# One border between two parts of a mixture-of-experts layer moved from row tile 36 to 40, scatters allowed between two gathers of a batch, and a wait rule of the planner changed

## The chip, the cores and the metric

The kernel runs on one core of one Trainium2 chip. The metric is the device time of one execution in microseconds, measured as the median of several runs. Beside it the profiler records one execution, whose rows are quoted below.

## The reference, cut to what matters

6250 nodes with 256 features go through one layer. `xn` is the layer norm of `x`. To `x` are added a graph term (for each of 106250 edges, sorted by destination, the row `xn[src]` times the edge's weight, summed by destination, times a 256x256 matrix) and a linear-attention term over all rows. The result goes through a second layer norm, a gate that picks 2 of 16 experts for each row, and the two chosen feed-forward experts (256 to 512, relu, 512 to 256):

```
agg = segment_sum(xn[src] * edge_weight[:, None], dst)
x   = x + agg @ weight + mix(xn)
y   = layernorm(x)
topk_vals, topk_idx = top_k(y @ gate_w + gate_b, 2)
h   = relu(y @ w1[e] + b1[e]);  expert_out = h @ w2[e] + b2[e]
out = x + layernorm(y + sum over the two chosen e of w * expert_out) * gamma + beta
```

## The kernel before, in words

The rows are cut into 49 row tiles of 128. The edges are cut into 831 tiles of 128 edges, and 12 of these make a batch; there are 70 batches (numbered 0 to 69, the last one with only 3 tiles). For each tile of edges GpSimd (POOL) issues one indirect DMA at L861 that gathers 128 rows of the normed table into `ring`. `ring` holds two batches, so the gathers of batch b wait at L859 for the products of batch b-2. TensorE forms the sums of a batch (`edges`, L1518), ScalarE copies them, TensorE puts them in place (`place`, L1527), and VectorE adds them into `aggT`. Since the edges are sorted by destination, row tile q is complete after batch `complete(q)` (35: batch 52, 39: batch 58, 47: batch 69, 48: batch 70, that is after the last one).

As row tiles become complete, groups of two of them go through `mix` (both added terms), `gate` (second norm and choice of experts) and, once for each sub-part of row tiles (`SUB`), through `rank`, `slots`, `line` and `list`. These count on VectorE, with small products on TensorE, which slot each row gets in a buffer that is sorted by expert. `slots` of a sub-part ends with `slots_done` (L1343, just after the copy at L1340). POOL then scatters the sub-part's rows into the slots, two indirect DMAs for each row tile (`scatter`, L839). `list` writes which expert and which tile of 128 slots each visit has. A visit (`moe`) is one tile of 128 slots through its expert: SP loads the expert's two weight blocks (514 KB at L738 and 640 KB at L740, only where the expert is new in its buffer of three) and the tile's rows (L727), TensorE transposes (L1642) and multiplies (`layer1` L1654 with 16 products, `layer2` L1667 with 8), VectorE adds the bias (L1451) and ScalarE's queue stores the result. After the last sub-part of a part (`PT`) everything that is still unvisited in that part is visited; before that only tiles that are full. Since the number of tiles is known only at run time, the last visits of a part's list are guarded: the list has a first run and a second, short run (`leave`) that is skipped as a whole when its first entry is empty. All engines go through `left_out` then.

When all visits of a part have stored their results, POOL picks them up row tile by row tile (`pick`, L852, two indirect DMAs for each row tile), and VectorE finishes the rows (`fin1`, `fin2`, L1469 to L1499) in groups of two row tiles. SP stores them (L770). In the kernel before no pick stands ahead of the end of the gathers.

The order of all this work is fixed when the program is written, by `plan()`. It walks through the batches with fixed costs (a gather 1.254, a visit 3.9, a scatter DMA 1.28, and so on) and fills, for each batch, the list `SLOTS[b]` of work that the engines do after the edges of batch b, and the list `POOL_AFTER[b]` of scatters and picks that POOL issues after the gathers of batch b. `SLOTS[70]` is the tail. Work of a batch may run over the planned landing of the next one by `LAG` = 6.0, except in the last three batches, where a visit is placed only if it ends before the landing. Within the tail no visit is placed ahead of the last sub-part's slots. `send(s, b, done)` places the scatter of sub-part s after the first batch whose planned landing is at least `SPARE` = 4.0 past the planned end of `slots`. `runs()` works out how many visits each sub-part lists.

With `SUB = (0, 8, 16, 24, 30, 36, 42, 49)` and `PT = (0, 36, 49)` the sub-parts list 8, 16, 16, 12, 32+3, 4 and 33+4 visits (a second number is the guarded `leave` run). Row tiles 0 to 35 are part 0, row tiles 36 to 48 are part 1.

Of the kernel before, what the change touches and what calls it, by code (L numbers as in the profile page):

```python
# [18 lines left out]
NT = NC * CH  # L19
# [13 lines left out]
BT = GT * WIN  # L33
TILES = -(-EDGES // P)
NB = -(-TILES // BT)
# [14 lines left out]

PT = (0, 36, NT)
SUB = (0, 8, 16, 24, 30, 36, 42, NT)
NPART, NSUB = len(PT) - 1, len(SUB) - 1
MOST = max(b - a for a, b in zip(SUB, SUB[1:]))
SUB_PART = [max(p for p in range(NPART) if PT[p] <= a) for a in SUB[:-1]]
PART = [max(p for p in range(NPART) if PT[p] <= q) for q in range(NT)]
ROWS_OF = [min(N, PT[p + 1] * P) - PT[p] * P for p in range(NPART)]

# [9 lines left out]
def ends_part(s):  # L70
    return SUB[s + 1] in PT


def runs():

    out, at = [], 0
    for p in range(NPART):
        seen, floors = 0, []
        for s in range(NSUB):
            if SUB_PART[s] != p:  # L80
                continue
            rows = min(N, SUB[s + 1] * P) - PT[p] * P
            mostly = max(0, 2 * rows // TS - MOSTLY)
# [29 lines left out]
MG = 2  # L113
GROUPS = [(a + i, min(a + i + MG, b)) for a, b in zip(SUB, SUB[1:]) for i in range(0, b - a, MG)]
FG = 2
# [19 lines left out]
GATHER, SCATTER = 1.254, 1.28  # L135
EDGES_PE, KV_PE, MID_PE, MIX_PE, GATE_PE, TAKEN_PE, LEFT_PE = 2.4, 5.0, 18.0, 2.3, 0.01, 3.9, 0.5
RANK_PE, LAG, SPARE, LANDS = 0.7, 6.0, 4.0, 4.0

BEHIND, TOP_DVE, SLOTS_DVE, LINE_DVE = (6.0, 5.0), (7.0, 4.0), (11.0, 8.5), (7.0, 4.5)
EDGE_SPARE = 5.0  # L140
# [6 lines left out]
def plan():  # L147
# [3 lines left out]
    pool = [[] for _ in range(NB + 1)]  # L151
    kvs, mixes, gates, routes = list(range(NT)), list(range(len(GROUPS))), [], []
    tiles, not_before, sent, over = [], {}, {}, {}
# [3 lines left out]
    def transfers(w):  # L157
        a, b = (SUB[w[1]], SUB[w[1] + 1]) if w[0] == "scatter" else FIN[w[1]]
        return 2 * (b - a) * SCATTER

    def landing(b, k):

        return landed + sum(GATHER * BT + sum(transfers(w) for w in pool[i]) for i in range(b, k))

    def send(s, b, done):

        k = b + 1
        while k < NB and landing(b, k) < done + SPARE:
            k += 1
        sent[s] = min(k, NB)  # L170
        at = max(done, landing(b, k) if k < NB else 0.0)
        pool[sent[s]].append(("scatter", s))
        not_before[s] = at + sum(transfers(w) for w in pool[sent[s]]) + LANDS

    def chain(work, b):
# [57 lines left out]
    for b in range(NB):  # L233
        landed = max(landed, edges_at[b]) + GATHER * BT
        now = max(now, landed) + EDGES_PE
        edges_at.append(now)
        work = slots[b]
        for f, at in opened:
            if at == b:
                work.append(("fin1", f))  # L240
        if fins and PART[FIN[fins[0]][0]] in over and over[PART[FIN[fins[0]][0]]] < b and b + 5 < NB:
            buffer = len(opened) % EB
            if free_from[buffer] <= b + 1:
                f = fins.pop(0)
                pool[b + 1].append(("pick", f))
                opened.append((f, b + 3))
                free_from[buffer] = b + 5
        while now < landing(b, b + 1) + (LAG if b < NB - ON_TIME else 0.0):
            before = now
            if kvs:  # L250
                work.append(("kv", kvs.pop(0)))
                now += KV_PE
                if not kvs:
                    slots[b + 1].append(("mid", 0))
                continue
            if ("mid", 0) in slots[b + 1]:
                break
            if work == [("mid", 0)]:
                now += MID_PE
            now += chain(work, b)  # L260
            if b < NB - ON_TIME or now + TAKEN_PE + AHEAD < landing(b, b + 1):
                now += expert(work, b)
            if now == before:
                then = next_time()
                if then is None or then > landing(b, b + 1) - EDGE_SPARE:
                    break
                now = then
        work += [("fin2", f) for f, at in opened if at == b]
        landed += sum(transfers(w) for w in pool[b])
    tail, end = slots[NB], pool[NB]  # L270
    waiting, closing, dve = [], [], 0.0
    while mixes or gates or routes or tiles or fins or waiting or closing:
        before = now
        if routes and routes[0][0] == "slots" and now >= routes[0][2]:
            s = routes[0][1]
            end.append(("scatter", s))
            sent[s] = NB
            landed = max(landed, now + SLOTS_DVE[1]) + transfers(end[-1])
            not_before[s] = landed + LANDS
        now += chain(tail, NB)  # L280
        if last in sent:
            before_tile = now
            now += expert(tail, NB)
            dve = max(dve, before_tile) + (RESULT_DVE if now > before_tile else 0.0)
            if closing and dve < now + CLOSE_DVE:
                tail.append(("fin2", closing.pop()))
                dve += CLOSE_DVE
            if not closing and waiting and waiting[0][1] <= now and dve < now + CLOSE_DVE:
                closing.append(waiting[0][0])
                tail.append(("fin1", waiting.pop(0)[0]))  # L290
                dve += CLOSE_DVE
        while fins and len(waiting) + len(closing) < TB - 1 and PART[FIN[fins[0]][0]] in over:
            f = fins.pop(0)
            end.append(("pick", f))
            landed = max(landed, now + (4.0 if PART[FIN[f][0]] == NPART - 1 else 0.0)) + transfers(end[-1])
            waiting.append((f, landed + 3.0))
        if now == before:
            now += 0.5
        assert now < 5000.0
    return slots, pool  # L300


SLOTS, POOL_AFTER = plan()
ORDER = [w for s in SLOTS for w in s]
MIXES = [w[1] for w in ORDER if w[0] == "mix"]
# [48 lines left out]
def gps_layer(nc, x, src, dst, first_dst, edge_w, gnn_w, wkv, wq, wout, bout, gate_w, gate_b,  # L354
# [5 lines left out]
    with ExitStack() as ctx:  # L360
# [250 lines left out]
        def after(eng, s, n):  # L611

            if n > 0:
                eng.wait_ge(s, n)  # L614
# [176 lines left out]
        def _(pool):  # L791
# [18 lines left out]
            for s, t in dealt.items():  # L810
                m = DEALT[s]
# [31 lines left out]
            def pick(f):  # L843
# [6 lines left out]
                for n, q in enumerate(range(*FIN[f])):  # L850
                    for k in range(2):
# [2 lines left out]
                            in_offset=bass.IndirectOffsetOnAxis(ap=slot_i[:, k, q:q + 1], axis=0),  # L854
                        ).then_inc(picked[i], 16)

            pool.wait_ge(consts_in, 16 * len(CONSTS))
            for b in range(NB):
                after(pool, batch_done, b - 1)  # L859
                for m in range(min(BT, TILES - b * BT)):  # L860
                    pool.indirect_dma_start(  # L861
                        out=ring[:, b % 2 * BT + m, :], out_offset=None, in_=table,
                        in_offset=bass.IndirectOffsetOnAxis(ap=src_sb[:, b * BT + m:b * BT + m + 1], axis=0),
                    ).then_inc(gathered[b % 2], 16)
                for stage in POOL_AFTER[b]:
                    {"scatter": scatter, "pick": pick}[stage[0]](stage[1])
            for stage in POOL_AFTER[NB]:
                {"scatter": scatter, "pick": pick}[stage[0]](stage[1])

        @block.scalar  # L870
        def _(act):
# [897 lines left out]
```

## Time and profile before

| what | value |
|---|---|
| time of the kernel, median of 3 runs | 1505.05 us (1502.7 to 1506.33) |
| time of the profiled execution | 1499.34 us |
| its span, first to last instruction | 1497.4 us |
| mean granted TensorE clock | 0.868 |
| PE busy / POOL busy | 1019.7 us / 1005.2 us |
| gathers, first start to last end | 53.2 to 1245.4 us |
| first scatter of the last sub-part | 1280.5 us |

The profiler's busy time is a share of the whole span, which has three stages here: a first one of norms (to 53 us), the gathers (to 1245 us), and the tail. An engine's share says little; what each stage waits for is read from the waits and from the timeline. In rows of the timeline the first number is the start and the second the duration in us, and the bracket at the end gives how long the engine was idle before the instruction and what released it.

### The profile page before, as it was taken

To read this page: it belongs to the slowest core of one execution; us is meant where nothing else is said; L and a number is where in the kernel's file an instruction comes from. 1 tells how busy PE (TensorE), PEld (TensorE's weight loads), DVE (VectorE), ACT (ScalarE), POOL (GpSimd) and SP (SyncE) were. 2 spreads that over 40 slices of the span, in tenths; PEclk is the share of its full clock that TensorE was granted. 3 is DMA by queue.
4 is the path that set the end of the run, shared out by engine and by line. 5 is a ranking of instruction groups with operands and counts; after the bars stand their busy time and mean duration, and the time that the engine had idled before them with its cause. 6 is when DMAs were issued, how large, how long until landed. Compare 5 with 4: busy or idle time off the path is not lost. (4 is left out here: it accounts for less than half of the span.)

```text
span 1497.4 us, 21938 instructions
## 1 busy us (share of the span) xinstructions
PE 1019.7 (68%) x6522; PEld 763.8 (51%) x6522; DVE 652.7 (44%) x2406; ACT 409.0 (27%) x1089; POOL 1005.2 (67%) x1094
## 2 busy tenths in 40 slices
PE   0099999997763889632599349636998674088960
PEld 0055555554542778521487238416887562077960
DVE  7445454453567413315213512341335233957307
ACT  4144343342122233101133113112333221033420
POOL 4477777777747777777777777777777756655015
PEclk9999999999886899956799779858999987589985
DMA  9576675633323898533698369538869753499754
GB/s 337 171 236 203 195 230 182 195 105 106 104 66 127 285 361 289 206 104 106 229 327 307 109 214 358 170 104 283 272 212 315 232 173 88 138 320 332 240 190 126
DMA packets 152445, 312.36 MB, mean 209 GB/s; under 512 B 24480, under 2 KB 97440, under 8 KB 152192
## 3 DMA queue, kind: packets, MB, share of 16 engines
q0 software_dynamic: 49296, 134.68, 28.7%
q1 hardware_dynamic: 63168, 137.52, 26.4%
q10 hardware_dynamic: 39856, 38.67, 7.7%
q8 instruction: 56, 0.92, 0.3%
q14 instruction: 69, 0.57, 0.1%
HBM read 246.42 MB, written 64.36 MB: 208 GB/s over the span
## 5 line engine op out<-in xcount | busy, mean ns | idle before, releaser
L861 POOL DMA_INDIRECT ring<-normed_rows,src_sb x831 | 796.0, 958 | 324.2 <-issue 287.7
L1654 PE MATMUL ps<-room 128*128 128x128 f32 x1888 | 245.9, 286 | 13.4 <-DMA room<-in_w1b 10.7
L1518 PE MATMUL ps<-ring,S 128*32 128x256 f32 x1680 | 129.6, 450 | 170.4 <-DMA ring<-normed_rows,src_sb 117.8
L1654 PEld LDWEIGHTS ps<-room 128*128 128x128 f32 x1888 | 235.0, 202 | 17.1 <-issue 10.1
L1667 PE MATMUL ps<-room 128*128 128x256 f32 x944 | 227.3, 384 | 8.6 <-issue 5.9
L1451 DVE TENSOR_TENSOR desk<-ps,room 128x256 f32<-128x256 f32 x121 | 51.2, 424 | 398.2 <-PE ps L1667 390.5
L1667 PEld LDWEIGHTS ps<-room 128*128 128x128 f32 x944 | 172.5, 193 | 30.5 <-issue 9.1
L1545 PE MATMUL ps<-room,tT 128*128 128x512 f32 x392 | 181.1, 606 | 0.0
L852 POOL DMA_INDIRECT ring<-results_by_slot,slot_i x98 | 95.9, 979 | 123.7 <-issue 104.3
L973 ACT ACTIVATE room<-ps,room 128x128 f32<-128x128 f32 x472 | 134.9, 368 | 132.9 <-PE ps L1654 132.8
L1518 PEld LDWEIGHTS ps<-ring,S 128*32 128x32 f32 x1680 | 57.2, 123 | 217.5 <-issue 185.2
L998 ACT COPY accs<-ps 128x256 f32<-128x256 f32 x70 | 26.1, 373 | 353.1 <-PE ps L1518 353.1
L839 POOL DMA_INDIRECT rows_by_slot<-X,slot_i x98 | 97.9, 999 | 34.2 <-issue 29.6
L1139 DVE TENSOR_REDUCE kv_var<-room 128x16 f32<-128x1024 f32 x49 | 59.8, 1220 | 133.0 <-ACT room L907 133.0
L1642 PE MATMUL ps<-ident,room 128*128 128x128 f32 x242 | 51.9, 299 | 90.3 <-issue 54.2
L1545 PEld LDWEIGHTS ps<-room,tT 128*128 128x128 f32 x392 | 73.1, 197 | 73.2 <-issue 73.2
L952 ACT COPY room<-ps 128x256 f32<-128x256 f32 x121 | 44.8, 370 | 208.6 <-DVE desk L1451 97.8
L1642 PEld LDWEIGHTS ps<-ident,room 128*128 128x128 f32 x242 | 32.4, 150 | 108.2 <-issue 81.4
L907 ACT ACTIVATE room<-ps 128x1024 f32<-128x1024 f32 x49 | 50.2, 1025 | 123.3 <-PE ps L1545 123.3
L1615 PE MATMUL ps<-M,tT 128*128 128x288 f32 x196 | 63.7, 452 | 2.2 <-issue 2.2
L1553 PEld LDWEIGHTS ps<-room 128*128 128x128 f32 x392 | 51.3, 191 | 23.9 <-issue 20.5
L1535 PE MATMUL ps<-ident,X 128*128 128x128 f32 x196 | 44.5, 312 | 27.1 <-ACT tT L887 26.2
(226 smaller groups left out, 1159.5 us busy)
## 6 DMA issues: line engine op xcount, KB each, us to landing
room<-in_w2b SPq DMA_DIRECT2D x83, 640.0 KB
room<-in_w1b SPq DMA_DIRECT2D x83, 514.0 KB, 5.7
room<-rows_by_slot SPq DMA_DIRECT2D x121, 128.0 KB
results_by_slot<-desk ACTq DMA_DIRECT2D x121, 128.0 KB
rows_by_slot<-desk ACTq DMA_DIRECT2D x6, 2432.0 KB
ring<-normed_rows,src_sb POOLq DMA_INDIRECT x831
normed_rows<-X SPq DMA_DIRECT2D x7, 896.0 KB, 8.0
result<-ring SPq DMA_DIRECT2D x49, 128.0 KB, 3.2
```

The costliest lines, as they stand in the source:

```text
L839: pool.indirect_dma_start(out=xs[p], out_offset=bass.IndirectOffsetOnAxis(ap=slot_i[:, k, q:q + 1], axis=0), in_=X2[:, q, :], in_offset=No ...
L852: pool.indirect_dma_start(out=pk[i][k][:, n, :], out_offset=None, in_=ys[p], in_offset=bass.IndirectOffsetOnAxis(ap=slot_i[:, k, q:q + 1], ...
L861: pool.indirect_dma_start(out=ring[:, b % 2 * BT + m, :], out_offset=None, in_=table, in_offset=bass.IndirectOffsetOnAxis(ap=src_sb[:, b * ...
L973: last = act.activation(hT[g % 2][:, f, :], hps[g % 2][:, f * TS:(f + 1) * TS], ACT.Relu, bias=w1_sb[g % WB][:, KD * F + f:KD * F + f + 1])
L1139: dve.tensor_reduce(kv_var[q % 2][:, :], sq.rearrange("p (h d) -> p h d", d=DH), AX.X, ALU.add).then_inc(kv_var_done, 1)
L1518: mm = pe.matmul(acc[w * W:(w + 1) * W, :], S[b % 2][:, m, :], ring[:, b % 2 * BT + m, :], start=(t == 0), stop=(t == GT - 1), skip_group_ ...
L1545: mm = pe.matmul(wide[q % 2][:, h * 512:(h + 1) * 512], tT[n % 2][:, k * P:(k + 1) * P], wkv_sb[:, k, h * 512:(h + 1) * 512], start=(k == ...
L1553: mm = pe.matmul(dotps[:, a, :], vs[q % 2][:, a * P:(a + 1) * P], ks[q % 2][:, a * P:(a + 1) * P], start=(q == 0 and a == 0), stop=False, ...
L1615: pe.matmul(lps_wide[n % 2], tT[t % 2][:, k * P:(k + 1) * P], M[:, k, :], start=(k == 0), stop=False, skip_group_check=True)
L1642: mm = pe.transpose(xgps[:, k * TS:(k + 1) * TS], xg[g % XB][:, k * P:(k + 1) * P], ident[:])
L1654: mm = pe.matmul(hps[g % 2][:, f * TS:(f + 1) * TS], w1_sb[g % WB][:, k * F + f * P:k * F + (f + 1) * P], xgT[g % 2][:, k, :], start=(k == ...
L1667: mm = pe.matmul(ops, hT[g % 2][:, f, :], w2_sb[g % WB][:, f * D:(f + 1) * D], start=(f == 0), stop=(f == FC - 1))
```

## The change

The border of the two parts moves from row tile 36 to row tile 40, and the sub-parts become (0, 8, 16, 24, 32, 36, 40, 49), so that part 1 is one sub-part of nine row tiles. In `send`, a scatter may stand inside a batch, after `into` of its gathers, if nothing else is placed after the batch ahead of it; `moves` issues it there. In the batches a step of a part's last routing (`gate` of its last group, `rank`, `slots`, `line`, `list`) may be waited for up to the planned landing of the next batch, where it was given up 5.0 ahead of it.

```diff
-PT = (0, 36, NT)
-SUB = (0, 8, 16, 24, 30, 36, 42, NT)
+PT = (0, 40, NT)
+SUB = (0, 8, 16, 24, 32, 36, 40, NT)
...
+        at, into = max(done, landing(b, k) if k < NB else 0.0), 0
         sent[s] = min(k, NB)
-        at = max(done, landing(b, k) if k < NB else 0.0)
-        pool[sent[s]].append(("scatter", s))
+        early = int((landing(b, k) - done - SPARE) / GATHER) if k < NB else 0
+        if 0 < early < BT and not pool[k - 1]:
+            sent[s], into, at = k - 1, BT - early, at - early * GATHER
+        pool[sent[s]].append(("scatter", s, into))
         not_before[s] = at + sum(transfers(w) for w in pool[sent[s]]) + LANDS
...
                 then = next_time()
-                if then is None or then > landing(b, b + 1) - EDGE_SPARE:
+                hurried = [ends_part(SUB.index(GROUPS[g][1]) - 1) for g, _ in gates if GROUPS[g][1] in SUB] + [ends_part(w[1]) for w in routes]
+                if then is None or then > landing(b, b + 1) - (0.0 if any(hurried) else EDGE_SPARE):
                     break
                 now = then
...
+            def moves(b, into):
+
+                for kind, i, m in POOL_AFTER[b] if b >= 0 else []:
+                    if m == into:
+                        {"scatter": scatter, "pick": pick}[kind](i)
...
             for b in range(NB):
                 after(pool, batch_done, b - 1)
                 for m in range(min(BT, TILES - b * BT)):
+                    if m:
+                        moves(b - 1, m)
                     pool.indirect_dma_start(
...
-                for stage in POOL_AFTER[b]:
-                    {"scatter": scatter, "pick": pick}[stage[0]](stage[1])
-            for stage in POOL_AFTER[NB]:
-                {"scatter": scatter, "pick": pick}[stage[0]](stage[1])
+                moves(b, 0)
+            moves(NB, 0)
```

## Rows read from the trace of the kernel before

**Rows 1.** The page: busy time, and the costliest groups.
```profile
PE 1019.7 (68%) x6522; PEld 763.8 (51%) x6522; DVE 652.7 (44%) x2406; ACT 409.0 (27%) x1089; POOL 1005.2 (67%) x1094
...
L861 POOL DMA_INDIRECT ring<-normed_rows,src_sb x831 | 796.0, 958 | 324.2 <-issue 287.7
L1654 PE MATMUL ps<-room 128*128 128x128 f32 x1888 | 245.9, 286 | 13.4 <-DMA room<-in_w1b 10.7
```

**Rows 2.** Waits of POOL: line, releaser, total us, times, longest.
```profile
POOL ring L861 <- PE ps L1518: 36.6, 8, 15.2
...
POOL rows_by_slot L839 <- DVEq L1343: 4.6, 1, 4.6
```

**Rows 3.** Timeline, 1185 to 1212 us: the longest gap of the late gathers.
```profile
1192.45 0.33 SPq L738 DMA_DIRECT2D room<-in_w1b  x1
...
1199.85 0.66 PE L1642 MATMUL ps<-ident,room 128*128 128x128 f32 x2 [11.79 <-DMA room<-rows_by_slot]
...
1211.62 0.95 POOL L861 DMA_INDIRECT ring<-normed_rows,src_sb  x1 [10.92 <-PE ps L1518]
```

**Rows 4.** Timeline, 1095 to 1125 us: visits and edges inside the gathers.
```profile
1099.62 0.42 DVE L1451 TENSOR_TENSOR desk<-ps,room 128x256 f32<-128x256 f32 x1 [3.31 <-PE ps L1667]
1103.35 0.42 DVE L1451 TENSOR_TENSOR desk<-ps,room 128x256 f32<-128x256 f32 x1 [3.31 <-PE ps L1667]
...
1121.38 1.50 PE L1518 MATMUL ps<-ring,S 128*32 128x256 f32 x24
1123.38 0.71 PE L1527 MATMUL ps<-Pm,accs 128*128 128x128 f32 x4 [0.49 <-ACT accs L998]
```

**Rows 5.** Timeline, last gather to first scatter of the last sub-part.
```profile
1244.45 0.95 POOL L861 DMA_INDIRECT ring<-normed_rows,src_sb  x1 [0.30 <-issue]
...
1248.55 1.50 PE L1518 MATMUL ps<-ring,S 128*32 128x256 f32 x24 [0.70 <-DVE aggT L1122]
...
1250.89 0.94 POOL L852 DMA_INDIRECT ring<-results_by_slot,slot_i  x1 [5.49 <-PE ps L1518]
...
1280.49 1.00 POOL L839 DMA_INDIRECT rows_by_slot<-X,slot_i  x1 [4.62 <-DVEq L1343]
```

**Rows 6.** Timeline, last scatter to last visit.
```profile
1297.69 1.08 POOL L839 DMA_INDIRECT rows_by_slot<-X,slot_i  x1 [0.30 <-issue]
1299.00 0.18 DVE L1443 SCALAR_TENSOR_TENSOR ttab<-ps,empty 1x37 int32<-1x37 f32 x1
...
1307.10 1.15 SPq L727 DMA_DIRECT2D room<-rows_by_slot  x2
...
1322.50 0.42 DVE L1451 TENSOR_TENSOR desk<-ps,room 128x256 f32<-128x256 f32 x1 [11.84 <-PE ps L1667]
...
1389.22 0.42 DVE L1451 TENSOR_TENSOR desk<-ps,room 128x256 f32<-128x256 f32 x1 [0.84 <-PE ps L1667]
...
1449.78 0.76 DVE L1451 TENSOR_TENSOR desk<-ps,room 128x256 f32<-128x256 f32 x2 [2.10 <-PE ps L1667]
```

**Rows 7.** Windows: stretch, length, busy us by engine, granted clock, DMA share, GB/s.
```profile
1312.70:1350.00 37.30, 34.14 (x219) 31.06 (x220) 23.11 (x68) 13.57 (x47) 22.25 (x23) 0.91 0.94 320
1350.00:1390.00 40.00, 33.65 (x228) 30.47 (x227) 31.09 (x94) 14.28 (x50) 18.62 (x20) 1.00 0.96 322
```

**Rows 8.** POOL's picks, 1298.9 to 1378 us grouped, then the last ones in time.
```profile
L852 POOL DMA_INDIRECT ring<-results_by_slot,slot_i x52 | 51.5, 990 | 27.3 <-issue 13.4 <-DMA results_by_slot<-desk 10.5 <-DMA result<-ring 3.4
```
```profile
1455.05 0.94 POOL L852 DMA_INDIRECT ring<-results_by_slot,slot_i  x1 [77.52 <-issue]
...
1487.02 0.95 POOL L852 DMA_INDIRECT ring<-results_by_slot,slot_i  x1 [0.30 <-issue]
...
1493.98 0.48 DVE L1499 SCALAR_TENSOR_TENSOR ring<-ring,f_r,aggT 128x256 f32<-128x256 f32 x1
```

**Rows 9.** Timeline, around the first scatter of sub-part 0.
```profile
456.25 0.18 DVE L1340 CAST slot_i<-slot_f 128x16 int32<-128x16 f32 x1
466.62 1.01 POOL L839 DMA_INDIRECT rows_by_slot<-X,slot_i  x1 [0.30 <-issue]
```

More of the change, by code:

```diff
@@ L244, in plan @@
                 f = fins.pop(0)
-                pool[b + 1].append(("pick", f))
+                pool[b + 1].append(("pick", f, 0))
                 opened.append((f, b + 3))
@@ L275, in plan @@
             s = routes[0][1]
-            end.append(("scatter", s))
+            end.append(("scatter", s, 0))
             sent[s] = NB
@@ L293, in plan @@
             f = fins.pop(0)
-            end.append(("pick", f))
+            end.append(("pick", f, 0))
             landed = max(landed, now + (4.0 if PART[FIN[f][0]] == NPART - 1 else 0.0)) + transfers(end[-1])
```

## The prediction

> **What bounds the kernel now.** I read the page first, then the waits of POOL, then timelines and windows of the late stages. By busy time no engine is full [rows 1]. POOL's 831 gathers at 0.958 us each, with 0.30 us to the next [rows 1, 5], follow each other every 1.25 us, so a full batch takes 15.0 us, and they set the pace from 53 to 1245 us. The reader should see in POOL's waits that in this stage it waits for TensorE only 36.6 us in 8 places [rows 2]; the last of them is 10.9 us before batch 67 [rows 3]. There TensorE itself had stood still for 11.8 us, waiting for the rows of the first visit of a new list: SP could issue these loads only once the guarded end of part 0's list had been passed over, and they started at 1192.45 us [rows 3]. The edges of batch 65 stood behind those visits, and the gathers of batch 67 wait for them.
>
> After the last gather (end 1245.4 us) comes a serial tail: last mix, gate, rank and slots to the first scatter, 35.1 us [rows 5]; 14 scatter DMAs to 1298.8 us and the start of the visits [rows 6]; 33 listed visits, the last two biases from 1449.8 us, which is 169.3 us past the first scatter [rows 5, 6]; then 26 picks of part 1 and the last rows' end, 47.6 us from 1449.8 to the span's end at 1497.4 us [rows 6, 8]. So the time is the gathers plus this tail, and TensorE matters only in the tail and where it holds up a batch.
>
> **Number of visits.** Which rows go to which expert follows from the inputs. Counting the reference's choices gives 82 slot tiles in part 0 and 36 in part 1 with the border at 36, together 118; 1888 products at 16 a visit are 118 visits [rows 1]. With the border at 40 the same count gives 89 and 28. `runs()` worked for the new borders lists 8, 16, 16, 16 and 8 visits, then 28+3 (25 of them real) and, for part 1, 29+4 (28 real).
>
> **The gathers.** The pre-tail scatters are 80 DMAs where they were 84: at (1297.69 - 1280.49)/13 = 1.32 us apart [rows 5, 6] -5.3 us. The stall of 10.9 us needs a short list of part 1 behind part 0's guarded end, in the middle of the gathers. There is none any more: part 1 has one sub-part, in the tail. I take the full -10.9 us; the bound is 0, if part 0's own visits now hold up the edges. I stepped through the planner's loop with its costs from batch 44 on. The last group of part 0 is mixed in batch 58, gated in 59 (rank in the same batch, by the new rule), slots end about 1019.6 on the planner's clock, and the 8 scatter DMAs go into batch 61 after 10 of its gathers. Batches 61 to 69 then get about 5, 4, 2, 3, 3, 2, 0, 2 and 1 visits, 22 of the 28. A visit takes 3.73 us in such a stretch, edges and place 2.2 us [rows 4]. Three visits and the edges are 13.4 of 15.0 us, so TensorE keeps up, and 25 visits need no switch of list. The first 5 visits begin some 11 us after the scatter, and their 19 us end about when the gathers two batches on ask for the edges: room about 2 us.
>
> **Scatters inside a batch** move POOL's work but add none. They use up slack: the scatter starts 4 to 5.3 us past the planned end of slots. Sub-part 0's slots were done at 456.5 and its scatter started at 466.62, 10.1 us of slack [rows 9], where the planner had counted 16.0. Moved ahead by 9 gathers (11.3 us), it would wait about 1.3 us, and sub-part 1's is of the same kind, some 2 us. Each gather behind waits with them. The visits start earlier, which may take something off the other small waits for TensorE, 25.7 us in all with 15.2 in one place [rows 2]. I take +1.5 us, with bounds -3 and +8.
>
> **From the last gather to the scatter.** New here: two visits in batch 68 stand ahead of the edges of batch 69, whose three gathers need only 3.75 us where the planner counts a whole batch. 7.5 us of visits against the 3 us that TensorE waits there now [rows 5] give +4.5. One visit between the last two mixes (3.73 us) gives +1.5, an estimate, as VectorE's adding of the last batch covers part of it. The routing of nine row tiles in place of seven widens its operations on VectorE by 9/7, an estimated +0.5. Sum +6.5 us, bounds 0 and +12. The 20 picks that POOL now issues in this stretch can't be issued any more, since part 0's last visits run only after rank; nor do they hold anything up today, as POOL waits 4.6 us for slots [rows 5].
>
> **From the scatter to the last visit.** The scatter is 4 DMAs longer, +5.3 us. Today the loads of the rows start at 1307.10, 8 us past the end of the scatter, with SP held at stores of early finished tiles and the list at 1299.0 [rows 6]. With no finished tiles at this point SP reaches the loads when the scatter has landed, so these 5 us are hidden; I take the first bias 42.0 us past the first scatter, as now (1322.50 - 1280.49 [rows 5, 6]), bounds 39 and 47. The 3 real visits left of part 0 and its guarded end fit on TensorE beside the 23 us of scatter; they keep the first picks back to its end at worst. Then 28 real visits in place of 32. While picks and finishes run beside them a visit takes (1389.22 - 1322.50)/15 = 4.45 us [rows 6]; afterwards (1449.78 - 1389.22)/16 = 3.79 us. All 80 picks of part 0 now come after the scatter, where 52 did: they took 78.7 us, 1.51 each with their waits [rows 8]. 80 of them take 100 us without and 120 us with such waits, so from 23 to about 133 us past the first scatter. That makes (133 - 42)/4.45 = 20.5 visits at the slow pace and some 6.5 at 3.79: 91 + 24.6, about 115.5 us for the visits, and the last bias at +157.5 where it is at +169.3. So -11.8 us. Bounds: all 27 steps at 3.98 us, the mean of now, -19; or 4.45 throughout and 5 us later start, +0.
>
> **Picks of part 1.** 18 in place of 26, at (1487.02 - 1455.05)/25 = 1.28 us [rows 8]: -10.2 us. POOL has been idle for 77.5 us when the first starts [rows 8], which leaves room for the 28 picks more of part 0 (42 us at 1.51). The last rows' end is as now.
>
> **Sum.** -5.3 - 10.9 + 1.5 + 6.5 - 11.8 - 10.2 = -30.2 us. The profiled execution took 1499.34 us, 5.7 us less than the median of 1505.05; the difference carried over to the median gives 1474.8, taken as 1475.0 us.
>
> **Rivals.** (A) The tail's transfers are the bound. In the slow stretch the DMA engines are busy 94 and 96% at 320 and 322 GB/s [rows 7], and more picks and stores now meet the visits there: 28 more picks and 14 more stores of 131 KB, 5.5 MB, at 322 GB/s 17 us of transfer, less 4 visits' rows and results (1 MB) and about three weight loads (3.5 MB), 3 us left. If also the loads crowd into the slow stretch, a visit takes 5.0 us there and the part is worth -1 in place of -11.8: sum -19, 1486 us. For it: the busy share. Against: TensorE waited only a few us for weights in all [rows 1]. The Trainium skill, "DMA: Bandwidth & Descriptors", section "Queues, rings and completion order", states that each engine takes turns between its queues packet by packet, so picks would slow the weight loads just so; the trace's slower pace beside the picks agrees, and by that rule the time would be rival A's.
>
> (B) The early part goes better: stalls go with the earlier visits and the last two visits in batch 68 cost nothing; +1.5 becomes -3, +6.5 becomes +1, visits -17: sum -45, 1460 us.
>
> (C) Part 0's crowded last list holds up every batch from 62 on, and the stall comes back spread out: the 10.9 us are not won and up to 8 more are lost, sum -19 to -11, 1490 us. For it: only 1.6 us of room in a batch with three visits.
>
> (D) Slower than before: the same mechanism with visits that wait for weights inside the gathers. At 3.73 us a batch has 1.6 us of room; -30 must be eaten by 22 visits plus that room in 8 batches (13 us), so it decides from 3.73 + 43/22 = 5.7 us a visit. The slowest pace of the trace, beside the picks, is 4.45. At 6 us: about +7, 1512 us.
>
> (E) The change doesn't do what it says: the border's move doesn't shorten the tail since the extra 6 us before the scatter and the slower start take all that visits and picks give, while the stall persists (+5.5, +11.8 and +10.9 on the sum): -2, about 1503 us.
>
> **How the numbers follow.** Forecast 0.60, A 0.16, B 0.10, C 0.07, E 0.03, D 0.04. A measurement here tells about 0.2% (3 us) from no change. Faster: all but D and most of E, 0.92; same 0.04; slower 0.04. The forecast's own range is 1467 to 1483; to hold 8 in 10 with A and part of B it is 1460 to 1490.
>
> **What would show it.** Gap before batch 67 gone (0.3 us), last gather's end near 1231; one or two waits of POOL for L1343 at the first two scatters, 1 to 3 us each; first tail scatter some 41 us past the last gather; 28 real visits, last bias near 157 us past that scatter; 18 picks after it. The prediction is wrong if new waits of L861 for L1518 of more than 5 us stand between batches 61 and 69, or if the visits of the tail take 5 us and PE waits for `in_w1b` far longer than the 10.7 us of now.

## The result, and the profile after

The changed kernel took 1493.81 us (median of 4 runs, 1489.54 to 1495.31) where the kernel before took 1505.69 us (median of 4, 1502.7 to 1509.21). The ratio is 0.9915, with an interval from 0.9889 to 0.994. So it gained 12.8 us by the ratio where 30.2 were forecast, and lies 3.8 us above 1490, the upper end of the wider of the two ranges. The profiled execution took 1489.54 us, its span is 1487.7 us. One of the nine executions of the run with the old border, below, took 2353.31 us where the other eight took 1511.82 to 1520.05; it is left out of that run's ratio.

The page of the kernel after: busy time, then the two groups that answer to [rows 1].

```profile
PE 1023.5 (69%) x6498; PEld 761.3 (51%) x6498; DVE 651.1 (44%) x2406; ACT 406.0 (27%) x1085; POOL 1007.7 (68%) x1094
...
L873 POOL DMA_INDIRECT ring<-normed_rows,src_sb x831 | 799.4, 962 | 326.0 <-issue 286.5
L1664 PE MATMUL ps<-room 128*128 128x128 f32 x1872 | 240.1, 284 | 17.8 <-DMA room<-in_w1b 17.0
```

The page can't tell where the time went: 1872 products are the 117 visits that were counted, and the gathers' busy time is 3 us more. In this kernel L873 is the gather, L843 the scatter, L856 the pick, L1461 a visit's bias, L1528 the edges, L1353 the end of `slots`. The waits of POOL in the kernel after (line, releaser, total us, times, longest) say more:

```profile
POOL ring L873 <- PE ps L1528: 39.5, 14, 15.1
POOL rows_by_slot L843 <- DVEq L1353: 47.8, 2, 44.8
```

Where 8 waits of gathers for TensorE were [rows 2], there are 14, and the sum has not fallen although the 10.9 us of [rows 3] are in it no longer. L1353 shows twice: 44.8 us is the tail's scatter, which now counts from the last gather, as no pick is issued ahead of it; 2.95 us is that of sub-part 0. The timeline of the kernel after around the first two scatters and the batches behind them:

```profile
461.12 0.18 DVE L1350 CAST slot_i<-slot_f 128x16 int32<-128x16 f32 x1
461.67 1.01 POOL L843 DMA_INDIRECT rows_by_slot<-X,slot_i  x1 [2.95 <-DVEq L1353]
...
497.03 1.00 POOL L843 DMA_INDIRECT rows_by_slot<-X,slot_i  x1 [2.19 <-issue]
...
516.21 0.97 POOL L843 DMA_INDIRECT rows_by_slot<-X,slot_i  x1 [0.30 <-issue]
...
541.11 0.42 DVE L1461 TENSOR_TENSOR desk<-ps,room 128x256 f32<-128x256 f32 x1 [12.96 <-PE ps L1677]
...
548.47 1.50 PE L1528 MATMUL ps<-ring,S 128*32 128x256 f32 x24
...
550.28 0.94 POOL L873 DMA_INDIRECT ring<-normed_rows,src_sb  x1 [4.28 <-PE ps L1528]
...
1247.84 0.95 POOL L873 DMA_INDIRECT ring<-normed_rows,src_sb  x1 [0.30 <-issue]
1248.77 2.79 PE L1528 MATMUL ps<-ring,S 128*32 128x256 f32 x24 [6.62 <-DMA ring<-normed_rows,src_sb]
...
1260.32 1.50 PE L1528 MATMUL ps<-ring,S 128*32 128x256 f32 x24
...
1293.63 1.00 POOL L843 DMA_INDIRECT rows_by_slot<-X,slot_i  x1 [44.83 <-DVEq L1353]
...
1333.68 0.42 DVE L1461 TENSOR_TENSOR desk<-ps,room 128x256 f32<-128x256 f32 x1 [21.26 <-PE ps L1677]
...
1452.45 0.76 DVE L1461 TENSOR_TENSOR desk<-ps,room 128x256 f32<-128x256 f32 x2
```

Three things are to be seen. First, scatters 0 and 1 wait 2.95 and 2.19 us, since POOL comes to them before their slots are ready (sub-part 0: cast at 461.12, scatter at 461.67), where sub-part 0's had waited for nothing [rows 9]. For sub-part 0 the scatter starts 0.37 us after the cast has ended. For sub-part 1 the profile names no releaser: its cast ended at 495.22 and the scatter started 1.8 us later, so that most of these 2.19 us is unexplained. (0.30 us of each is the usual distance between two DMAs.) Second, the last scatter of sub-part 1 ends at 517.2, but the first visit of its list has its bias only at 541.11, 24 us on. The plan set 8 visits into batch 25, the last four of them from this list, and three of these (541.11 to 548.58) stand ahead of the edges of batch 26 at 548.47; the gathers of batch 28 wait 4.28 us for those edges. TensorE's clock has a share in the delay. TensorE stood idle for 1.56 us before 528.19, and in 530 to 532 us its granted clock was 0.50, the lower of its two levels (1.2 GHz). In the mean of 528 to 541 us it was 0.74, and the 16 products of layer 1 took 3.57 and 3.07 us, where the next 16 (541.13, clock 1.00) took 1.95. The kernel before has 0.74 in that stretch too. Third, the edges of batch 69, 3.15 us past the last gather before [rows 5], come 11.5 us past it now (1260.32 - 1248.79).

To find where time is lost among 831 gathers, I took the gathers' start times by batch and subtracted 1.2525 us for each gather and 1.275 us for each scatter DMA (what they take back to back). What is left is time in which POOL stood still. The kernel before was profiled twice, and so was the one after (both are in the experiments); these are means of the two:

| us | before | after | difference | forecast |
|---|---|---|---|---|
| standing still, batches 0 to 24 | 23.7 | 25.9 | +2.2 | 0 |
| batches 25 to 30 | 3.1 | 11.4 | +8.3 | +1.5 for all scatters inside a batch |
| batches 31 to 56 | 8.1 | 12.2 | +4.1 | (in the line above) |
| batches 57 to 61 | 1.5 | 4.0 | +2.5 | 0 |
| batches 62 to 69 | 11.8 | 1.0 | -10.8 | -10.9 |
| four scatter DMAs fewer | | | -5.1 | -5.3 |
| last gather to first tail scatter | 34.1 | 44.8 | +10.8 | +6.5 |
| first tail scatter to last bias | 168.6 | 158.8 | -9.8 | -11.8 |
| last bias to the end of the span | 47.6 | 35.2 | -12.4 | -10.2 |
| sum | | | -10.2 | -30.2 |

Two profiles of one kernel differ by up to 7 us in standing still (44.6 and 51.7 for the kernel before, 52.9 and 55.9 for the one after). Single lines differ by up to 3.0 us for the kernel before and by 5.4 us for the one after (9.5 and 14.9 in batches 31 to 56), so a line of a few us means little unless a wait of a known cause or several profiles stand behind it.

### The profile page after: what moved, and what is told of

It reads as the page before. It is cut to its first block and busy times, and to the rows that moved or that the text cites. A ratio compares the mean times of both kernels' runs of the same rounds, so it can differ in the third digit from the quotient of the medians.

```text
span 1487.7 us, 21903 instructions
## 1 busy us (share of the span) xinstructions
PE 1023.5 (69%) x6498; PEld 761.3 (51%) x6498; DVE 651.1 (44%) x2406; ACT 406.0 (27%) x1085; POOL 1007.7 (68%) x1094
## 5 line engine op out<-in xcount | busy, mean ns | idle before, releaser
L873 POOL DMA_INDIRECT ring<-normed_rows,src_sb x831 | 799.4, 962 | 326.0 <-issue 286.5
L1528 PE MATMUL ps<-ring,S 128*32 128x256 f32 x1680 | 133.8, 462 | 233.0 <-DMA ring<-normed_rows,src_sb 148.2
L1664 PE MATMUL ps<-room 128*128 128x128 f32 x1872 | 240.1, 284 | 17.8 <-DMA room<-in_w1b 17.0
L1664 PEld LDWEIGHTS ps<-room 128*128 128x128 f32 x1872 | 228.4, 199 | 22.9 <-issue 20.6
L1528 PEld LDWEIGHTS ps<-ring,S 128*32 128x32 f32 x1680 | 58.8, 126 | 281.4 <-issue 252.6
L1461 DVE TENSOR_TENSOR desk<-ps,room 128x256 f32<-128x256 f32 x121 | 51.2, 424 | 330.6 <-PE ps L1677 324.7
L1677 PEld LDWEIGHTS ps<-room 128*128 128x128 f32 x936 | 171.6, 194 | 30.9 <-issue 12.0
L1555 PE MATMUL ps<-room,tT 128*128 128x512 f32 x392 | 177.4, 595 | 0.0
L843 POOL DMA_INDIRECT rows_by_slot<-X,slot_i x98 | 96.1, 981 | 78.9 <-DVEq L1353 47.8
L856 POOL DMA_INDIRECT ring<-results_by_slot,slot_i x98 | 96.8, 988 | 65.8 <-issue 49.0
L962 ACT COPY room<-ps 128x256 f32<-128x256 f32 x121 | 44.6, 369 | 173.3 <-PE ps L1652 97.7
L1625 PE MATMUL ps<-M,tT 128*128 128x288 f32 x196 | 68.5, 481 | 1.3 <-ACT tT L897 1.3
L1180 DVE SCALAR_TENSOR_TENSOR X<-X,std,bout_b 128x256 f32<-128x256 f32 x49 | 23.0, 483 | 105.3 <-PE ps L1545 105.3
L1563 PEld LDWEIGHTS ps<-room 128*128 128x128 f32 x392 | 52.4, 195 | 23.5 <-issue 20.7
L1545 PE MATMUL ps<-ident,X 128*128 128x128 f32 x196 | 45.2, 316 | 25.9 <-ACT tT L897 25.4
```

Of the source, the lines that this page charges most:

```text
L843: pool.indirect_dma_start(out=xs[p], out_offset=bass.IndirectOffsetOnAxis(ap=slot_i[:, k, q:q + 1], axis=0), in_=X2[:, q, :], in_offset=No ...
L856: pool.indirect_dma_start(out=pk[i][k][:, n, :], out_offset=None, in_=ys[p], in_offset=bass.IndirectOffsetOnAxis(ap=slot_i[:, k, q:q + 1], ...
L873: pool.indirect_dma_start(out=ring[:, b % 2 * BT + m, :], out_offset=None, in_=table, in_offset=bass.IndirectOffsetOnAxis(ap=src_sb[:, b * ...
L1461: dve.tensor_tensor(yo[g % 2], ops, w2_sb[g % WB][:, W2ROW:], ALU.add).then_inc(y_done, 1)
L1528: mm = pe.matmul(acc[w * W:(w + 1) * W, :], S[b % 2][:, m, :], ring[:, b % 2 * BT + m, :], start=(t == 0), stop=(t == GT - 1), skip_group_ ...
L1555: mm = pe.matmul(wide[q % 2][:, h * 512:(h + 1) * 512], tT[n % 2][:, k * P:(k + 1) * P], wkv_sb[:, k, h * 512:(h + 1) * 512], start=(k == ...
```

## The experiments

Each edit is against the changed kernel, in `plan()` or in the two lines of the borders. The ratios are against the kernel before, run beside each of them. "Inside" is short for scatters between two gathers of a batch.

| variant | median us | ratio, interval |
|---|---|---|
| border only | 1490.24 | 0.9908, 0.9876 to 0.994 |
| no scatter inside | 1488.44 | 0.9891, 0.986 to 0.9923 |
| old border | 1513.14 | 1.0067, 1.004 to 1.0095 |
| inside for part 0's last sub-part only | 1485.78 | 0.9891, 0.9857 to 0.9925 |
| inside, with 6 us more of margin | 1489.18 | 0.9909, 0.9877 to 0.9941 |
| inside, visits not placed earlier | 1489.74 | 0.993, 0.9904 to 0.9956 |
| last sub-part only, batches 68 and 69 free | 1485.63 | 0.9894, 0.9862 to 0.9926 |
| inside for sub-parts 2 to 5 | 1491.06 | 0.9922, 0.9892 to 0.9952 |
| last sub-part only, later visits | 1476.79 | 0.9823, 0.9782 to 0.9863 |
| the changed kernel, again | 1492.24 | 0.9935, 0.9909 to 0.996 |
| last sub-part only, again | 1482.7 | 0.9877, 0.9839 to 0.9915 |

**The border alone.** No scatter inside a batch, and the old rule for a part's last routing.

```diff
-        if 0 < early < BT and not pool[k - 1]:
+        if False:
...
-                if then is None or then > landing(b, b + 1) - (0.0 if any(hurried) else EDGE_SPARE):
+                if then is None or then > landing(b, b + 1) - EDGE_SPARE:
```

> The border moves alone: no scatter inside a batch, no waiting for a part's last routing. 19 of the 28 visits of part 0's last list are planned ahead of the tail where the changed kernel has 22. Theory 1 (scatters inside batches cost the gathers what the border wins): the last gather ends near 1235 us on the profile's clock in place of 1248.8, and the kernel is 20 to 26 us faster than before; the 3 visits more in the tail hide beside the 23 us of its scatters. Theory 2 (the new small waits of the gathers come with the new border itself): about as the changed kernel, 12 us faster than before. Theory 3 (visits ahead of the tail are what counts): 3 visits of 3.73 us more in the tail, so at most 5 us faster than before.

Measured: 0.9908, no worse than the whole change. In its profile POOL stands still 1.1 us in batches 25 to 30 and 1.3 us in 62 to 69, so the stall before batch 67 goes with the border alone. What the wait rule for a part's last routing does shows in the tail: only 19 visits were placed ahead of it, three fewer, and from first tail scatter to last bias it takes 176.8 us in place of 158.8. The timeline of this kernel shows an idle stretch of POOL ahead of a pick of part 0, some 37 us past the first tail scatter. The profile names no releaser for it; the last biases of that part's visits are at 1313 to 1316 us, and a pick waits for all of them:

```profile
1319.57 0.99 POOL L856 DMA_INDIRECT ring<-results_by_slot,slot_i  x1 [14.61 <-issue]
```

In the times the rule can't be told: this kernel and the next one, which has it, are 1.8 us apart, well inside their intervals.

**No scatter inside a batch, the rest as in the change.**

```diff
-        if 0 < early < BT and not pool[k - 1]:
+        if False:
```

> The changed kernel with every scatter after a whole batch again; border and wait rule as changed, 22 visits ahead of the tail as in the changed kernel. Theory 1: the waits around batches 24 to 28 (some 9 us) and the two waits of POOL for the slots (2.9 and 2.2 us) go, the last gather ends near 1237 us, 22 to 26 us faster than before. Theory 2: no different from the changed kernel, 12 us faster than before.

Measured: 0.9891. All 22 visits still stand ahead of the tail. The profiled execution stood still 49.3 us, 4 to 7 less than the changed kernel in its two. The interval overlaps that of the change, so this run alone doesn't decide. Of the 20 to 26 us that theory 1 gave for these two runs and for the one with a single scatter inside, 13.8, 16.4 and 16.4 came.

**The old border with the two new rules.**

```diff
-PT = (0, 40, NT)
-SUB = (0, 8, 16, 24, 32, 36, 40, NT)
+PT = (0, 36, NT)
+SUB = (0, 8, 16, 24, 30, 36, 42, NT)
```

> The kernel before with scatters inside batches and the new wait rule, border at 36 as before. Theory 1: 5 to 12 us slower than before, with the same growth of small gaps at batches 24 to 28 as in the changed kernel. Theory 2: within 3 us of before.

Measured: 1.0067, slower than before by 10 us, and the whole interval is a loss. With the border out of play, the two other rules together cost 10 us. The wait rule has little part in that: worked through `plan()`, at this border it moves no scatter and no visit, only steps of the routing in batches 52 to 55. The profile of this run shows standing still of 10.5 us in batches 25 to 30 (3.1 before), and sub-part 0's scatter waits there too:

```profile
457.70 1.00 POOL L843 DMA_INDIRECT rows_by_slot<-X,slot_i  x1 [1.94 <-DVEq L1353]
```

In batches 31 to 56, where the scatters of sub-parts 2 to 4 are inside batches too, it stands still 7.9 us, no more than the kernel before (8.1).

**A scatter inside a batch only where it ends a part.**

```diff
-        if 0 < early < BT and not pool[k - 1]:
+        if 0 < early < BT and not pool[k - 1] and ends_part(s):
```

> The changed kernel with a scatter inside a batch only for the last sub-part of part 0 (after 11 gathers of batch 61); 22 visits ahead of the tail. Theory 1: like the version with no scatter inside a batch, 22 to 26 us faster than before, since one gather of 1.25 us is all that it moves. Theory 2: like the changed kernel, 12 us faster than before.

Measured: 0.9891. Standing still in batches 25 to 30 is 2.3 us, and the last gather starts at 1234.02 where it was 1247.84. The same kernel was run again beside the changed one later.

**Inside, but with more margin for the slots.** The scatters of sub-parts 0 and 1 come after 8 and 5 gathers, in place of 3 and 1.

```diff
-        early = int((landing(b, k) - done - SPARE) / GATHER) if k < NB else 0
+        early = int((landing(b, k) - done - SPARE - 6.0) / GATHER) if k < NB else 0
```

> The changed kernel with scatters inside a batch started 6 us later than it places them (10 us past the planned end of the slots in place of 4), which leaves only sub-parts 0 and 1 inside a batch, after 8 and 5 gathers. Theory 1a (POOL stands waiting for slots that VectorE finishes some 6 us later than planned): the two waits of POOL for the slots go, and the gathers of batch 30 start about 5 us earlier than in the changed kernel. Theory 1b (the visits that follow earlier hold up the edges of batches 25 to 27): the gap before batch 28 or 29 stays at 4 us or more and batch 30 starts within 3 us of the changed kernel. Time by 1a 1.3% less than before, by 1b 1.0% less.

**Inside, but visits placed as if the scatter came after the whole batch.**

```diff
-            sent[s], into, at = k - 1, BT - early, at - early * GATHER
-        pool[sent[s]].append(("scatter", s, into))
-        not_before[s] = at + sum(transfers(w) for w in pool[sent[s]]) + LANDS
+            into = BT - early
+        pool[k - 1 if into else sent[s]].append(("scatter", s, into))
+        not_before[s] = at + sum(transfers(w) for w in pool[k - 1 if into else sent[s]]) + LANDS
```

> The changed kernel with the scatters inside batches at the same places, but the visits that follow them placed as if the scatter came after the batch. Theory 1a (waits for slots): nothing improves, batch 30 starts within 2 us of the changed kernel, 0.85% less than before. Theory 1b (visits too early): the gap of 4.3 us before batch 28 goes and batch 30 starts 4 us earlier, time 1.2% less than before.

These two take the cost apart. With more margin the wait for the slots is gone (0.30 us), but the wait before batch 28 stays:

```profile
464.83 1.01 POOL L843 DMA_INDIRECT rows_by_slot<-X,slot_i  x1 [0.30 <-issue]
...
546.56 0.94 POOL L873 DMA_INDIRECT ring<-normed_rows,src_sb  x1 [5.44 <-PE ps L1528]
```

With later visits it is the other way round: the scatter waits, and between 470 and 590 us no gather waits over 0.8 us for TensorE. The granted clock is 1.00 from 528 to 541 us, where it was 0.74. One wait comes up further on, 2.52 us before batch 31, where the changed kernel had 1.90 before batch 30 and 0.69 before batch 31. (The last scatter of part 0 moved by one gather with this edit, to 11 gathers into batch 61.)

```profile
462.05 1.01 POOL L843 DMA_INDIRECT rows_by_slot<-X,slot_i  x1 [2.95 <-DVEq L1353]
...
562.35 0.95 POOL L873 DMA_INDIRECT ring<-normed_rows,src_sb  x1 [0.73 <-PE ps L1528]
```

In batches 25 to 30 both stand still 8.1 to 8.3 us, 3 less than the changed kernel: each removes one of the two waits. Their times, 0.9909 and 0.993, can't be told from the changed kernel's: what each half is worth is read from the profiles alone.

**Batches 68 and 69 without visits**, with one scatter inside.

```diff
-        if 0 < early < BT and not pool[k - 1]:
+        if 0 < early < BT and not pool[k - 1] and ends_part(s):
...
-            if b < NB - ON_TIME or now + TAKEN_PE + AHEAD < landing(b, b + 1):
+            if b < NB - ON_TIME or b < NB - 2 and now + TAKEN_PE + AHEAD < landing(b, b + 1):
```

> The version with a scatter inside a batch only for the last sub-part of part 0, with no visits in batches 68 and 69: their 3 visits move into the tail. Theory 4 (these visits only delay the tail's start): the first tail scatter comes 8 us earlier after the last gather (38 us in place of 46), and since 22 us of scatter hide two or three of the visits the kernel gains 3 to 6 us on that version. Rival 5 (part 0's last visits are the tail's own chain, as the version with the border alone suggests, whose visits of part 1 begin 52 us past the scatter in place of 42): the visits of part 1 start at the same time on the clock or later, and nothing is gained, 0 to 5 us lost.

Measured: 0.9894, the same as with those visits, so the 3 to 6 us of theory 4 didn't come. The timeline of this kernel shows that the edit did what it was meant to:

```profile
1240.12 0.96 POOL L873 DMA_INDIRECT ring<-normed_rows,src_sb  x1 [0.30 <-issue]
1279.77 1.00 POOL L843 DMA_INDIRECT rows_by_slot<-X,slot_i  x1 [38.70 <-DVEq L1353]
```

The stretch from the last gather to the scatter is 38.7 us in place of 42.6 to 46.9 in the other kernels with the new border. But the visits that were taken out run behind the scatter, whose last bias is then 168.1 us on, where it was 162.5 in the same kernel with them. What is won ahead of the scatter is paid behind it: the longer stretch is no loss by itself.

**The kernel before, once more** (one execution).

> The kernel before, unchanged, for a second profile of it. If a profile's last gather varies by less than 2 us (1245.4 us in the first), the differences of 5 us and more between the versions are theirs; if it varies by 5 us, only sums over several profiles tell them apart.

Measured: 1503.96 us, 4.6 us more than its first profiled execution. The last gather starts at 1252.55, 8.1 us later than in [rows 5], with nearly the same tail (33.0 to the scatter, 167.9 and 47.6 behind it). The wait before batch 67 is there, with 11.5 us. So the last gather of one kernel came 8 us apart in two executions, of which the shorter tail gave 3.5 back, and the forecast had taken all its numbers from a single one.

**Scatters 0 and 1 after their batches, 2 to 5 inside.**

```diff
-        if 0 < early < BT and not pool[k - 1]:
+        if 0 < early < BT and not pool[k - 1] and s >= 2:
```

> The changed kernel with the scatters of sub-parts 0 and 1 after whole batches; those of 2 to 5 stay inside. Theory 1 (the cost lies in the two 16-DMA scatters that follow each other): POOL's excess in batches 25 to 30 falls from about 11 to 3 us, the rest stays, 1.1 to 1.2% faster than before. Rival: scatters inside batches 38, 49, 56 and 61 cost as much again, 0.9%.

Measured: 0.9922, nothing that can be told from the changed kernel beside it (1492.24 us, last rows of the table), and 8 us slower than the version with one scatter inside (1482.7), though its standing still in batches 25 to 30 is only 3.9 us. In batches 31 to 56 it is 13.7 us. That the two scatters whose slots are late are the whole cost falls with this run: by the times, the scatters of sub-parts 2 to 4, which wait for nothing, cost inside their batches about as much as those of 0 to 4 did together. By the profiles this is less sure: 31 to 56 have 9.5, 14.9 and 13.7 us in the three profiles with these scatters inside and the visits placed with them, 6.9 to 9.8 in the five with whole batches, but also only 7.9 with the old border. Why the costs of the two sets don't add up is open.

**Visits placed from 10 us past the scatter** (in place of `LANDS`) for all but a part's last sub-part, and one scatter inside.

```diff
-        if 0 < early < BT and not pool[k - 1]:
+        if 0 < early < BT and not pool[k - 1] and ends_part(s):
...
-        not_before[s] = at + sum(transfers(w) for w in pool[sent[s]]) + LANDS
+        not_before[s] = at + sum(transfers(w) for w in pool[sent[s]]) + (LANDS if ends_part(s) else 10.0)
```

> The version with a scatter inside a batch only for the last sub-part of part 0, and with the first visits of every other sub-part placed 6 us later after its scatter (10 us in place of 4), as the traces show the first visit begins some 11 us after it. Theory 6 (the small gaps of the gathers come from visits that stand in a batch's list before they can begin): POOL's excess over back-to-back work in batches 57 to 61 falls from 4 to 6 us to under 2, in 25 to 56 from about 10 to 7, and the kernel is 5 us faster than that version, 1.4% faster than before. Rival: the work is only moved on and the excess comes in the batches behind, no difference.

Measured: 0.9823, the fastest of all, faster than the kernel before by 26.6 us and than the changed one too. The edit also moved part 0's last scatter by two gathers, from 11 gathers into batch 61 to 1 into batch 62. POOL's waits in this kernel:

```profile
POOL ring L873 <- PE ps L1528: 35.6, 5, 15.1
```

Five waits where the changed kernel has 14. One is new (9.25 us before batch 29), but in batches 31 to 61 POOL stands still 3.6 us, where it was 11.1 and 11.9 in the two profiles with one scatter inside and the old distance. With the new wait, batches 25 to 56 come to 12.9 us, not to the 7 that were expected. The profiled execution (1484.01 us) was the slowest of its six (1469.05 to 1484.01), and over all batches it stands still 44.9 us, more than the 39.0 and 40.7 of the two with one scatter inside. So the profile doesn't show where its lead comes from. Over the kernel with one scatter inside (0.9877, next) it leads by 5.9 us; the intervals overlap, and so do the runs (1469.05 to 1484.01 against 1480.25 to 1487.33).

**The changed kernel and the one with one scatter inside, again**, on the same chip.

> The changed kernel again, beside the others on one chip: 0.85% faster than before as measured first, with POOL's excess of about 11 us in batches 25 to 30 again.

> The version with a scatter inside a batch only for the last sub-part of part 0 again, beside the changed kernel: by theory 1 it is 5 to 8 us faster than that, 1.1 to 1.3% faster than before; if scatters inside batches cost nothing, the same.

Measured: 1492.24 us (12 runs, 1487.0 to 1498.09) against 1482.7 us (6 runs, 1480.25 to 1487.33), ratios 0.9935 and 0.9877: 8.7 us apart by the ratios, 9.5 by the medians, and the slowest run of the second is about the fastest of the first. The waits of POOL for the edges, first of the changed kernel, then of the other:

```profile
POOL ring L873 <- PE ps L1528: 42.9, 14, 15.1
```
```profile
POOL ring L873 <- PE ps L1528: 33.4, 9, 15.3
```

## Why the prediction was wrong, step by step

**Scatters inside a batch: the step that failed.** Without it the forecast's wide range would have held: the kernel with one scatter inside took 1482.7 us. The prediction took "+1.5 us, with bounds -3 and +8". Measured are +8.6 us in batches 25 to 30 (11.4 against 2.7, the mean of the five profiles with the new border and whole batches for these scatters) and +4.2 in batches 31 to 56 (12.2 against 8.0), together 12.8 us in profiles (where the second number is the weak one) and 8.7 us in the times of the last two runs; the old border gives 10 us. In batches 25 to 30 it has two halves:
- The waits before the scatters: forecast 1.3 and some 2 us, measured 2.95 and 2.19, of which 0.30 each is the usual distance. So 4.5 us for 3.3; this half was sized about right, and more margin removes it.
- The visits: I wrote that they "start earlier, which may take something off the other small waits". They do the opposite. A scatter issued earlier makes the planner put its visits into an earlier batch, from `LANDS` past its end. But the first bias of a list comes far behind that: 24 us past the last scatter of sub-part 1, 20.8 us for sub-part 4 in the changed kernel (1045.9 to 1066.68), and 17.5 us for the scatter that ends at 1019.3 in the kernel before. With the plan ahead of the work, TensorE comes to visits that can't start or run slowly, the next edges stand behind them, and the gathers two batches on wait. For batches 25 to 30 this is shown: with the same scatters and later visits the wait of 4.28 us before batch 28 goes. For the sub-parts behind them it is argued from there. It is rival C's mechanism, but in the sub-parts before the last list, where I had looked for it.

The lead bought nothing: with the scatters of sub-parts 0 to 4 after whole batches all 22 visits still stand ahead of the tail. At most 3 to 5 us come back there, as last gather to end of span is 238.9 us in the changed kernel and 242 to 244 in those.

**The stall before batch 67: right.** -10.9 forecast; -10.8 in batches 62 to 69, and it needs only the border, as the first and third run show (with the old border it stays, 11.6 us there). In the five profiles of the other new-border kernels batches 62 to 69 still hold 3.0 us in the mean, 6.2 in one. Neither of the two signs that the prediction gave for being wrong came: no new wait of a gather in batches 61 to 69 of the changed kernel is over 1.20 us, and a visit of the tail doesn't take 5 us. The loss was where no sign had been set. Part of what the stall gave is paid in batches 57 to 61, though: 4.7 us in the mean of the five new-border profiles where 1.5 was, which the forecast had at nothing. It had looked at this place ("room about 2 us") for the last list only.

**Fewer scatters and the count of visits: right.** -5.1 against -5.3; 117 visits, 22 of 28 placed ahead of the tail.

**Last gather to first tail scatter: 10.8 for 6.5.** The two visits in batch 68 were to cost 4.5 us; they cost 8.5 in the mean of the two pairs of profiles (11.5 against 3.15 in the first pair, 11.5 against 2.8 in the second). I let TensorE start them while the last gathers were issued, but they stand behind the edges of batch 68, and those wait 6.62 us for their own rows, till 1248.77. Both visits therefore lie wholly behind the last gather. Some 1.9 us of the 8.5 are these rows themselves: the edges of batch 68 began 1.9 us before the last gather's end in both profiles of the kernel before and 0.02 us before it in both of the one after. The rest of this stretch grew by 2.2 us, where 2.0 were forecast. As the run without these visits shows, they would cost as much behind the scatter.

**Scatter to last bias, and the picks: right in sum.** -9.8 for -11.8, and -12.4 for -10.2. The first real bias of part 1 is 40.05 us past the scatter in the first profile and 43.05 in the second (42.0 taken), and 27 steps take 118.8 and 115.7 us (115.5 taken). The end that comes out at the forecast to 1.3 us is in part two deviations that cancel. The bound of -19 was worked out with 3.98 us a step as "the mean of now"; from 1322.50 to 1449.78 are 31 steps, 4.11 us each, which makes it -16; nothing rests on it.

**Rival A is not borne out.** The DMA engines are as busy as it says. Windows of the same stretch, after, then before (stretch, length, TensorE busy with its matmuls, granted clock, DMA share, GB/s):

```profile
1330.00:1440.00 110.00, 98.72 (x652) 0.98 0.94 322
```
```profile
1330.00:1440.00 110.00, 100.18 (x684) 1.00 0.85 277
```

But TensorE's waits for what they bring are short. In the kernel after, 1324 to 1452 us:

```profile
PE ps L1664 <- DMA room<-in_w1b: 7.0, 6, 1.7
PE ps L1652 <- DMA room<-rows_by_slot: 4.5, 4, 1.7
```

Ten waits of at most 1.7 us, six for weights and four for a visit's rows, and a step of 4.46 us in the mean while picks run (1333.68 to 1436.29, 23 steps), as forecast, against the 5.0 that this rival needs there. The time came out near this rival's and C's (1486 and 1490), but the loss sits in the gathers.

**What stays open.** Some 2 us more of standing still before batch 25 appear in all profiles with the new border but one, and in the second profile of the kernel before too; I hold that for variation but haven't shown it. What scatters of sub-parts 2 to 4 inside a batch cost, and by which waits, differs from profile to profile and was not taken apart by a run of its own. Whether 10 us is the best distance for the visits was not tried, nor why the one wait of 9.25 us comes up with it. The prediction took 0.2% (3 us) as the least difference that a measurement shows; the interval of the change is 0.26% to each side, and those of the experiments up to 0.4%.

## What to carry to other kernels

A transfer that is issued earlier helps only if what waits for it is late; where a fixed order also moves its consumers forward, ask from when they can really run (here the first bias came 15 to 24 us past the transfer's end, where the plan had 4 and a visit of 3.9) and what is queued behind them. Measure that distance in the trace before anything is made tighter. A step towards it in the planner (10 us in place of 4) went with the fastest kernel here, though its lead of 5.9 us over the same kernel without it is within what the runs overlap. And a forecast of 2% for a kernel whose gathers end 8 us apart from one execution to the next needs more than one profile of it.

## What the runs showed of the hardware

- One kernel on one core varied more than I had allowed for: the kernel before took 1495.11 to 1509.95 us in 20 runs side by side with other kernels, and its last gather started at 1244.45 us in one profile and at 1252.55 in another, with the same work.
- With the DMA engines 94% busy at 322 GB/s beside them, a visit took 4.40 us in the mean (4.29 in the second profile), against 3.73 us inside the gathers [rows 4]. TensorE's waits for transfers are 11.5 us of the 18 us that this makes in 27 steps. VectorE is 84 us of 110 busy there too, with the finishing of rows, so the rest isn't assigned.
- In the changed kernel TensorE stood idle 1.56 us before 528.19, inside the gathers; its granted clock was 1.00 in 524 to 528 us and 0.50 in 530 to 532, and 16 products took 3.57 us in place of 1.95. So a wait of TensorE can cost more than its own length.
